# A decoder layer on one core: another order of the cross-attention's spectra, queries ahead of the last turn of the mixing, context's sums behind the last head roots

## What is computed

```python
# end of the first part: gates mix five branches, a norm by head, a projection
o = w_ctx[..., 0:1] * short + w_ctx[..., 1:2] * long_ + w_ctx[..., 2:3] * wide + w_ctx[..., 3:4] * delta_out + w_val * v
o = o * jax.lax.rsqrt(jnp.mean(o * o, -1, keepdims=True) + 1e-05) * onorm_w
return o.reshape(b, Ll, HID) @ o_w.T
...
x = _layernorm(x + _L0_attn_ref(x, ...))
...
# cross-attention of x (queries) with ctx (keys and values), 16 heads of 16
qf = jnp.fft.rfft(q, axis=1)
kf = jnp.fft.rfft(k, axis=1)
corr = jnp.fft.irfft(qf * jnp.conj(kf), n=L, axis=1).mean(axis=-1)
corr = corr.transpose(0, 2, 1)
weights, delays = jax.lax.top_k(corr, topk)
w = jax.nn.softmax(weights, axis=-1)
idx = (jnp.arange(L)[None, None, None, :] - delays[..., None]) % L
v_h = v.transpose(0, 2, 1, 3)
gathered = jnp.take_along_axis(v_h[:, :, None], idx[..., None], axis=3)
out = (w[..., None, None] * gathered).sum(axis=2)
...
return out @ Wo.T + bo
```

## Time and profile before

| | us |
|---|---|
| median of three timed executions | 693.91 (693.59 to 694.21) |
| the profiled execution, its time | 689.84 |
| its span, from first to last instruction | 688.0 |
| TensorE busy | 579.3 (84%) |
| VectorE busy | 456.1 (66%) |
| ScalarE busy | 283.0 (41%) |
| GpSimd (POOL) busy | 117.3 (17%) |
| granted TensorE clock, mean | 0.953 of 2.4 GHz |

### The profile page before, as it was taken

The page is one execution under the profiler, slowest core; times in us unless marked ns, Lnnn a source line. Parts: engine busy times, 40 slices in busy tenths (PEclk is TensorE's granted clock), DMA queues, the critical chain, the costliest instruction groups (busy, mean ns, idle before and its releaser), DMA issues. The chain is left out here.

```text
span 688.0 us, 16960 instructions
## 1 busy us (share of the span) xinstructions
PE 579.3 (84%) x7436; PEld 420.8 (61%) x7448; DVE 456.1 (66%) x890; ACT 283.0 (41%) x518; POOL 117.3 (17%) x102
## 2 busy tenths in 40 slices
PE   5768679999999999898986767699999758988984
PEld 2445466777768677776543446588787644555642
DVE  2973458767685786873858899354566854576664
ACT  1874534433443344333354532343324054544531
POOL 1001340150042006010011224372000010000000
PEclk9999899999999999998999978999999888999988
DMA  6601420240041004132410017000000000000001
GB/s 176 214 1 43 145 93 3 81 137 5 3 155 64 4 16 142 34 95 88 159 62 0 31 30 236 30 1 1 0 1 1 0 0 1 1 30 1 31 12 51
DMA packets 26537, 37.51 MB, mean 55 GB/s; under 512 B 4641, under 2 KB 13602, under 8 KB 26463
## 3 DMA queue, kind: packets, MB, share of 16 engines
q1 hardware_dynamic: 26463, 36.42, 16.4%
HBM read 34.31 MB, written 2.10 MB: 53 GB/s over the span
## 5 line engine op out<-in xcount | busy, mean ns | idle before, releaser
L298 DVE SCALAR_TENSOR_TENSOR arena<-bank,conv_w,arena 128x511 f32<-128x511 f32 (+2 forms) x72 | 53.2, 746 | 29.8 <-ACT arena L1097 14.1
L1479 POOL COPY arena<-v_win 128x256 f32<-128x256 f32 x32 | 20.1, 650 | 178.0 <-PE bank L744 178.0
L1932 ACT COPY arena<-bank 128x512 f32<-128x512 f32 x40 | 23.3, 585 | 55.5 <-PE bank L1735 36.0
L1735 PE MATMUL bank<-v_win,arena 128*128 128x256 f32 x192 | 45.2, 384 | 0.0
L2507 PE MATMUL bank<-v_win,arena 128*128 128x256 bf16 x288 | 36.5, 279 | 7.9 <-DVE arena L2594 7.0
L744 PE MATMUL bank<-arena 128*32 128x128 f32 x512 | 35.7, 409 | 6.8 <-ACT arena L1108 6.3
L1158 ACT COPY arena<-bank 128x512 f32<-128x512 f32 x40 | 21.5, 590 | 46.4 <-PE bank L866 46.4
L1735 PEld LDWEIGHTS bank<-v_win,arena 128*128 128x128 f32 x192 | 36.8, 193 | 5.3 <-issue 0.4
L2497 PE MATMUL bank<-arena,v_win 128*128 128x512 bf16 x134 | 36.2, 400 | 3.7 <-DVE arena L2565 3.2
L2507 PEld LDWEIGHTS bank<-v_win,arena 128*128 128x128 bf16 x288 | 28.4, 100 | 16.7 <-DVE arena L2594 7.9
L1113 ACT COPY arena<-bank 128x256 f32<-128x256 f32 x32 | 19.3, 602 | 46.8 <-PE bank L757 46.7
(11 more groups left out here) (275 smaller groups left out, 1343.9 us busy)
## 6 DMA issues: line engine op xcount, KB each, us to landing
arena<-in_toep_w SPq DMA_DIRECT2D x32, 256.0 KB, 2.9
arena<-in_toep_l SPq DMA_DIRECT2D x32, 256.0 KB, 3.6
arena<-in_xT SPq DMA_DIRECT2D x12, 512.0 KB, 4.4
arena<-in_x SPq DMA_DIRECT2D x4, 512.0 KB, 3.8
arena<-in_ctx SPq DMA_DIRECT2D x4, 512.0 KB, 4.4
out<-arena SPq DMA_DIRECT2D x4, 512.0 KB, 2.9
qkv_w<-in_qkv_wT SPq DMA_DIRECT2D x1, 768.0 KB, 5.5
v_win<-in_w_gateT SPq DMA_DIRECT2D x1, 768.0 KB, 4.4
```

Of the source, the lines that this page charges most:

```text
L298: return nc.vector.scalar_tensor_tensor(out=acc[:, j:L], in0=src[:, 0:L - j], scalar=conv_w[:, m, CONV_K - 1 - j:CONV_K - j], in1=acc[:, j:L],
L1735: i = mm(oo, src[:, k, f * P:(f + 1) * P], w[:, k, :], start=(k == 0), stop=(k == KT - 1 and f > 0))
L1932: nc.scalar.copy(dst(i), bank[RING_FIRST + n % RING].rearrange("p (t c) -> p t c", c=dst(i).shape[-1]))\
```

## The change

`ORDER` names the twenty spectra in the order in which they are made, and `spectrum` numbers them by it, so that the ring of PSUM banks follows any order. TensorE's list and ScalarE's are then written in another order, `sums` moves on VectorE, and `ctx_sums(0)` moves on POOL. Each engine still does the same operations on the same data.

```diff
--- before.py
+++ after.py
@@ -1546,8 +1546,9 @@
         turn3_bank = lambda b, k: bank[(1, 5 if b < B - 1 else 0)[k]]
 
         PAIRS, PW = B // 2, 2 * COLS
-        KINDS = ("x", "c", "q", "k", "v")
-        SPECTRA = 2 * len(KINDS)
+        ORDER = [(0, "x"), (0, "q"), (1, "x"), (0, "c"), (0, "k"), (0, "v"), (1, "c"), (1, "q"), (2, "x"), (1, "k"), (1, "v"),
+                 (2, "c"), (2, "q"), (3, "x"), (2, "k"), (2, "v"), (3, "c"), (3, "q"), (3, "k"), (3, "v")]
+        SPECTRA = 2 * len(ORDER) // B
         RING, RING_FIRST = 4, 2
         A4 = carve(arena, {"xeo": (2, TT * D), "ctx": (2, TT * D), "ceo": (2, TT * D)})
         at4 = lambda at, *shape: carve(arena, {"it": shape}, at=at)["it"]
@@ -1590,7 +1591,7 @@
 
         def spectrum(b, kind, i):
 
-            return SPECTRA * b + 2 * KINDS.index(kind) + i
+            return 2 * ORDER.index((b, kind)) + i
 
         hd = lambda x: x.rearrange("p e (h c) -> p e h c", c=XD)
 
@@ -1831,38 +1832,39 @@
                         hidden(b + 2, 1)
                     if b == B - 2:
                         pe.wait_ge(late_loaded.sem, 16 * 5)
-                        forward_x(0)
                     turn_o(b)
                     if b < B - 2:
                         hidden(b + 2, 2)
+                    else:
+                        forward_x(0)
                     project(b)
                     if b < B - 2:
                         hidden(b + 2, 3)
                         logits(b + 2)
                         turn_logits(b + 2)
-                forward_ctx(0)
-                turn_o(B - 1)
                 pe.wait_ge(dc_loaded.sem, 16 * 3)
                 project_q(0)
+                turn_o(B - 1)
+                forward_x(1)
+                forward_ctx(0)
                 project(B - 1)
                 project_k(0)
                 project_v(0)
-                forward_x(1)
                 forward_ctx(1)
                 project_q(1)
+                forward_x(2)
                 project_k(1)
                 project_v(1)
-                forward_x(2)
                 forward_ctx(2)
                 project_q(2)
                 correlation(0)
+                forward_x(3)
                 project_k(2)
                 project_v(2)
-                forward_x(3)
+                forward_ctx(3)
                 turn_delays(0)
-                forward_ctx(3)
+                project_q(3)
                 forward_delays(0)
-                project_q(3)
                 project_k(3)
                 project_v(3)
                 inverse(0)
@@ -2006,36 +2008,37 @@
                         norm_out(b - 1)
                     if b < B - 2:
                         gelu(b + 2, 1)
+                    if b < B - 1:
+                        turned_out(b)
                     if b == B - 2:
                         x_out(0)
-                    if b < B - 1:
-                        turned_out(b)
                     if b < B - 2:
                         gelu(b + 2, 2)
                     if b < B - 1:
                         mix_squares(b + 1)
+                    if b == B - 2:
+                        q_out(0)
                     if b < B - 2:
                         gelu(b + 2, 3)
                         logits_out(b + 2)
+                turned_out(B - 1)
+                x_out(1)
                 ctx_out(0)
-                turned_out(B - 1)
-                q_out(0)
                 k_out(0)
                 norm_out(B - 1)
                 v_out(0)
-                x_out(1)
                 ctx_out(1)
                 q_out(1)
+                x_out(2)
                 k_out(1)
                 v_out(1)
-                x_out(2)
                 ctx_out(2)
                 q_out(2)
                 evens_out(0)
+                x_out(3)
                 k_out(2)
                 exps(0)
                 v_out(2)
-                x_out(3)
                 ctx_out(3)
                 q_out(3)
                 k_out(3)
@@ -2356,11 +2359,11 @@
                 residual(B - 1)
                 shift(B - 1)
 
+                sums(2)
                 products(0)
-                sums(2)
+                sums(3)
                 products(1)
                 coefficients(0)
-                sums(3)
                 best(0)
                 products(2)
                 delays_turned(0)
@@ -2431,11 +2434,10 @@
                 pool.wait_ge(s3["last_red"].sem, 5)
                 g.tensor_tensor(late_of(1), late_of(1), half_up, ALU.pow).then_inc(s3["last_root"].sem, 1)
                 for b in range(B):
-                    if b == B - 1:
-                        ctx_sums(0)
                     head_roots(b)
                     if b:
                         norm_roots(b - 1)
+                ctx_sums(0)
                 ctx_sums(1)
                 norm_roots(B - 1)
                 pool.wait_ge(s3["x1_out"].sem, s3["x1_out"].at(B - 1, 4))
```

## The result

The change makes the kernel slower, by about as much as was forecast. In 17 timed executions of each, it took 697.03 us (median; 692.13 to 701.15) against 693.84 us (691.02 to 697.38): ratio 1.0043, with an interval of 1.0022 to 1.0064, or +1.5 to +4.4 us. The medians are 3.2 us apart; the forecast was +2.5.

The account below looks back on a forecast made before the run. Bound by VectorE, slowed by POOL, up to T, then TensorE nearly level with a VectorE chain up to S, which sets the end. Terms -1.96 + 3.54 - 0.98 + 1.87 = +2.5, so 696.4 us; range 692.3 to 697.9.

Parts of the forecast that it names:

- T: Start of turn_o(3), the last turn of the mixing; forecast 1.96 us earlier, at 434.53, as weigh(3)'s last sums end sooner.
- What stays: At shift and head_norm POOL's sums still hold VectorE up; POOL's third queued operation does not do so again.
- (b): Ahead of T, VectorE takes shift and both halves of head_norm before POOL's sums; 692.4 us with clock up; chance 0.10.
- (c): POOL's third operation precedes head_norm's second half; T and S 1.26 us later; 695.8, or 697.6 at low clock; chance 0.10.
- Ahead of T: TensorE's work there is done by 428.3, over 6 us before T, covered by the wait for VectorE; costed at nothing.
- F: Start of the step behind forward_delays(0); forecast T + 67.45 + 3.54 = 505.52 us, 1.58 later than before.
- S: Start of correlation(1); forecast 519.82, 14.30 us behind F and 0.6 later than before, with TensorE waiting 3.0 for VectorE.
- (d): TensorE bounds up to S, everything behind T moves with it: -2.3, 691.6 us; chance 0.03 with anything else faster.
- The clock: Behind the new gap TensorE's clock reads 0.50, slowing the 16 rows of correlation(1): +1.87 us, ends 0 and 2.3.
- (a): The clock stays up over the gap ahead of correlation(1): +0.6, 694.5 us, no difference that can be told; chance 0.32.
- The end follows S: Behind correlation(1) the lists are the same in both kernels, so the end moves as S moves.

Follow-up runs that it names:

- old_tail_sums_late: The change with everything behind correlation(0) in the old kernel's order, and GpSimd waiting for head_norm(3) before ctx_sums(0) and (1); 691.36 us, ratio 0.9961; again 690.51, 0.9940.
- q3_ahead_only: The kernel before the change with project_q(3) put ahead of forward_delays(0), nothing else; 698.85 us, ratio 1.0074.
- q3_behind: The change with project_q(3) put back behind forward_delays(0) on TensorE, nothing else; 694.22 us, ratio 0.9996.
- old_tail: The change with everything behind correlation(0) in the old kernel's order on TensorE and ScalarE, VectorE's list kept; 691.94 us, ratio 0.9983.
- sums_ahead: The change with ctx_sums(0) put back ahead of head_roots(3) on GpSimd; 699.02 us, timed once.

## Why the prediction was right

By its own steps, in us behind W, measured in the profile of the change against what the text had:

- **T.** 1.59 earlier, forecast 1.96. This term was mis-sized, and the step is "L2151 can start at 423.01 - 0.45 + 0.1". The 0.45 us of idleness ahead of L2151 was put down to POOL; it is there (0.46) in every kernel, with POOL idle too. What causes it is open. The excess of the two sums alone, 2.89 - 1.29 = 1.60, is the gain.
- **What stays.** `shift` and `head_norm(3)` held up by 2.1 us, POOL's third operation behind VectorE: as written. Rival (b) needed them to go first, (c) the third ahead; neither happened. `old_tail_sums_late` shows that the 2.1 us were there to be had.
- **Ahead of T.** TensorE waits 7.72 us there with q in front: its cover is ample, as said.
- **F.** T-F 70.71, forecast 70.99.
- **S.** F-S 14.46, forecast 14.30; a wait of 3.00, forecast 3.0. `q3_ahead_only` shows that the place of q(3) makes it; (d) is out.
- **The clock.** 1.39 (4.13 - 2.74), forecast 1.87, ends 0 and 2.3. It fell behind each of the three gaps of 3.00 in these runs, at 1.39, 1.66 and 1.66, so (a) is out for all that was seen. The Trainium skill (TensorE: Matmul & The Clock Gate, "Why this matters for your kernels") warns only of gaps longer than about this, and read to the letter would have let these go free; the three runs disagree.
- **The end follows S.** S-I is 21.70 or 21.68 in all eight profiles of the table with the clock up at S.

Set against each other, the terms were off by +0.37 (T), -0.28 (T to F), +0.16 (F to S) and -0.48 (the clock), which leaves the +2.24 of the stretches against +2.47. Each term is within half a microsecond, so the mechanism was right; that they cancel to 0.23 is luck, and so is much of how near T-F came, since it scatters by 1.6. What the forecast did not see is that x(3) ahead of `exps(0)`, and the delay steps with little between them, have a price too. In the change q(3) hides both; they show only once it is moved (`q3_behind`), and as `old_tail` puts both back at once, their shares are known only from the rows there: 0.38 us of waiting, and 1.69 lost between F and S at the low clock.

## What to carry to other kernels

Where two engines' chains reach the same point within a microsecond, count both before moving a step: q(3), moved on TensorE's list, gave TensorE no more work, but it delayed the start of VectorE's chain by its whole length. Work moved ahead of a wait pays only up to the next place where another engine is late; measure from marks inside the program, since here the opening alone scatters by more than the change is worth. An operation that is in no hurry, such as POOL's sums here, is worth holding behind a semaphore where it would hold up another engine's chain.

## What the runs showed of the hardware that I had not expected

The clock fell behind a stretch in which TensorE was almost never idle: 3.3 us of matmuls with 64 and 32 columns and a wait of 0.38 (`q3_behind`). With a transform of 256 columns between the two steps and no wait it stayed at 1.00 (`old_tail`); which of the two differences decides was not separated. And back-to-back operations are not alike on the two engines that hold each other up: VectorE's held POOL's add for 4.16 us in `sums_ahead` (1.26 undisturbed). It began beside one 1024-wide operation, stood through the next two, and ended 1.13 us behind the last of them, in and just behind VectorE's pause of 0.46; in the kernel before it was the same (3.71 us, 1.12). POOL's four in a row let a waiting VectorE in after one.
